# Routed experts of an AdaLN block on one core: one wait per gather and per adding scatter on GpSimd, the scatters' order kept by ScalarE, the expert register loaded one block ahead

## What is computed

```
scores = softmax(x @ gate_w.T)                      # 16 experts
topk_w, topk_ids = top_k(scores, 6); topk_w /= topk_w.sum()
for each expert e:  out += c_e[:, None] * (silu(x @ w1_e.T) * (x @ w3_e.T)) @ w2_e.T     # width 176
out += swiglu(x, shared weights)                     # width 352
result = x + gb * out
```

## Time and profile before

| | us |
|---|---|
| runs, median of 2 (lowest, highest) | 730.74 (729.31, 732.18) |
| profiled execution, its time | 729.74 |
| profiled execution, span from first to last instruction | 727.9 |
| busy in that span: TensorE / VectorE / ScalarE / GpSimd | 657.0 / 389.5 / 346.7 / 496.0 |
| mean granted TensorE clock | 0.95 |

### The profile page before, as it was taken

The page is one execution under the profiler, slowest core; times in us unless marked ns, Lnnn a source line. Parts: engine busy times, 40 slices in busy tenths (PEclk is TensorE's granted clock), DMA queues, the critical chain, the costliest instruction groups (busy, mean ns, idle before and its releaser), DMA issues.

```text
span 727.9 us, 13620 instructions
## 1 busy us (share of the span) xinstructions
PE 657.0 (90%) x4053; PEld 477.9 (66%) x4053; DVE 389.5 (54%) x1240; ACT 346.7 (48%) x886; POOL 496.0 (68%) x455
## 2 busy tenths in 40 slices
PE   8999997999989999965899999999999999999904
PEld 7889996999879988744565655555555555555503
DVE  6988779989777867897323222222222222222206
ACT  4788798989989654210244432332233233223300
POOL 4578878770876310598787888888788787878640
PEclk8999999999999999986899999999999999999965
DMA  8000001393001129100355555555555555554459
GB/s 308 2 1 1 2 1 45 103 322 88 2 1 37 38 77 288 37 13 0 92 91 82 86 87 86 84 86 90 82 85 89 86 82 88 90 82 84 67 82 314
DMA packets 55716, 61.55 MB, mean 85 GB/s; under 512 B 7800, under 2 KB 49024, under 8 KB 55520
## 3 DMA queue, kind: packets, MB, share of 16 engines
q0 software_dynamic: 21312, 30.02, 25.4%
q1 hardware_dynamic: 33920, 30.07, 13.4%
q10 hardware_dynamic: 416, 0.59, 0.2%
HBM read 37.18 MB, written 23.48 MB: 83 GB/s over the span
## 4 chain that ended last, share of the span: by engine, by line
PE 44%; POOL 24%; issue 15%; DMA 7%; DVE 4%; ACT 3%; SPq 1%; POOLq 0%; DVEq 0%; ACTq 0%
POOL xg L678 9%; PE ps L1453 7%; POOL routed L684 6%; POOL qoh L671 6%; DMA routed<-yb,idx 5%; PE ps L1097 4%; PE ps L1470 3%; PE ps L1303 3%; PE ps L1469 2%; PE ps L1444 2%; PE ps L1224 2%; PE ps L1248 2%; PE ps L1235 2%; PE ps L1249 2%; PE ps L1264 2%
## 5 line engine op out<-in xcount | busy, mean ns | idle before, releaser
L684 POOL DMA_INDIRECT routed<-yb,idx x111 | 176.0, 1586 | 39.3 <-issue 31.1
L1979 DVE SCALAR_TENSOR_TENSOR sw<-sil,cwt,ps 128x176 f32<-128x176 f32 x111 | 44.1, 398 | 250.9 <-ACT sil L986 250.9
L1453 PE MATMUL ps<-up_w,gT 128*128 x444 | 159.7, 483 | 8.2 <-ACT gT L980 4.1
L992 ACT ACTIVATE yb<-ps 128x256 f32<-128x256 f32 x111 | 42.7, 384 | 211.0 <-DMA routed<-yb,idx 188.4
L678 POOL DMA_INDIRECT xg<-token_rows,idx x111 | 110.6, 996 | 37.4 <-issue 30.2
L1453 PEld LDWEIGHTS ps<-up_w,gT 128*128 128x128 f32 x444 | 76.4, 192 | 49.8 <-issue 26.2
L1470 PE MATMUL ps<-dn,swT 48*128 x222 | 77.3, 428 | 0.0
L1469 PE MATMUL ps<-dn,swT 128*128 x222 | 66.4, 381 | 1.6 <-ACT yb L992 1.6
L671 POOL TENSOR_SCALAR qoh<-iota,blkf,tokn 128x112 f16<-128x112 f16 x48 | 40.8, 864 | 35.9 <-DVE blkf L1886 35.9
L986 ACT ACTIVATE sil<-ps,zero 128x176 f32<-128x176 f32 x111 | 45.6, 411 | 25.5 <-PE ps L1453 25.5
L1470 PEld LDWEIGHTS ps<-dn,swT 48*128 48x128 f32 x222 | 32.7, 184 | 36.8 <-issue 36.8
(11 more groups left out here) (275 smaller groups left out, 1418.6 us busy)
## 6 DMA issues: line engine op xcount, KB each, us to landing
up_w<-in_moew SPq DMA_DIRECT2D x4, 1408.0 KB, 12.7
routed<-zrow SPq DMA_DIRECT2D x2, 2176.0 KB, 16.2
accb<-routed SPq DMA_DIRECT2D x8, 512.0 KB, 8.1
wog<-combine SPq DMA_DIRECT2D x2, 1024.0 KB, 6.8
token_rows<-hxb SPq DMA_DIRECT2D x8, 256.0 KB, 2.2
out<-x1T SPq DMA_DIRECT2D x8, 256.0 KB, 2.3
xg<-token_rows,idx POOLq DMA_INDIRECT x111, 2.8
routed<-yb,idx POOLq DMA_INDIRECT x111
```

Source lines behind the costliest of these rows:

```text
L684: po.indirect_dma_start(acc_d[k % 2][:, :], bass.IndirectOffsetOnAxis(ap=idx[:, k:k + 1], axis=0), yb[:, k % Y_BUFS, :], None, compute_op= ...
L1453: last = mm(up_block(j), gT[:, j % 2, kc, :], up_w[:, kc, :, bass.ds(expert[j], 1), :], start=(kc == 0), stop=(kc == KC - 1))
L1979: ve.scalar_tensor_tensor(out=sw[:, j % 2, 0:I], in0=sil[:, j % 2, :], scalar=cwt[:, j % 4:j % 4 + 1], in1=up_block(j)[:, 1, :], op0=ALU.m ...
```

## The change

Four edits. `fetch(i)` has one wait in place of two: for `sw` of block i-6 (`s_a`), which comes after `x_t` and `c_ok` of that block. `add_rows(k)` has one wait in place of two: for `yb` k alone. ScalarE's yb(j) waits, from j = 2 on, for the landing of scatter j-2 in place of scatter j-4, and so keeps the order that `add_rows` kept before. TensorE loads the expert's register of block j+1 behind the up matmuls of block j, and not ahead of those of block j+1.

```
             def fetch(i):
                 if i >= XG_BUFS:
-                    po.wait_ge(*late("x_t", i + 1 - XG_BUFS))
-                    po.wait_ge(*late("c_ok", i + 1 - XG_BUFS))
+                    po.wait_ge(*late("s_a", i + 1 - XG_BUFS))
                 po.indirect_dma_start(xg[:, i % XG_BUFS, :], None, hx_d[:, :], ...)

             def add_rows(k):
                 po.wait_ge(*late("s_y", k + 1))
-                if k >= 2:
-                    po.wait_ge(S[f"sc{k % 2}"], 16 * (k // 2))
                 po.indirect_dma_start(acc_d[k % 2][:, :], ..., yb[:, k % Y_BUFS, :], None, compute_op=ALU.add)...

                     ac.wait_ge(*late("s_dn", j + 1))
-                    if j >= Y_BUFS:
-                        ac.wait_ge(S[f"sc{j % 2}"], 16 * ((j - Y_BUFS) // 2 + 1))
+                    if j >= 2:
+                        ac.wait_ge(S[f"sc{j % 2}"], 16 * (j // 2))
                     ac.activation(yb[:, j % Y_BUFS, :], bank(6 + j % 2)[:, 0:D], ACT.Copy).then_inc(S["s_y"], 1)

-            expert = {}
+            expert = {0: pe_.value_load(tab[0:1, 0:1], min_val=0, max_val=E - 1)}
...
                 if 0 <= j < NB:
-                    expert[j] = pe_.value_load(tab[j:j + 1, 0:1], min_val=0, max_val=E - 1)
                     pe_.wait_ge(*late("g_t", j + 1))
...
                     last.then_inc(S["s_up"], 1)
+                    if j + 1 < NB:
+                        expert[j + 1] = pe_.value_load(tab[j + 1:j + 2, 0:1], min_val=0, max_val=E - 1)
```

## The result

The changed kernel takes 768.23 us (median of two executions, 765.53 and 770.93) against 730.74: 1.052 times as long, 95% interval 1.0477 to 1.0564. Five further rounds gave 771.44 (769.99 to 774.76) against 729.45: 1.0575, 1.0545 to 1.0604. The direction and the mechanism were as forecast; the size was not. The range of 741 to 768 ends just under the first median and 3 us under the second, and the profiled execution (770.93) is 41.2 us over the one before (729.74) where the sum said 26.9.

The account below looks back on a forecast made before the run. GpSimd's own 3.19 us per block was taken as the bound. Start +3.7, loop +24.8 and end -1.6 summed to 26.9 us on the profiled 729.74, or 756.6; the forecast was 757 us, range 741 to 768.

Parts of the forecast that it names:

- What bounds the kernel before: Mid loop, GpSimd is its own bound: scatter 1.59, gather 1.00, two gaps of 0.30, 3.19 us per block; TensorE needs 2.79.
- Second waits for nothing: Taking second waits off GpSimd's 222 gathers and scatters gains 0 us each; the 0.30 us gap stays.
- The single wait at 0.29: On GpSimd, a gather with one wait starts 0.29 us after `sw` is done, priced from scatter 0.
- Rival C: The gather's single wait for `sw` costs 0.74 us, not 0.29: 780 us, chance 0.09.
- The register load at nothing: Moving 111 register loads on TensorE's queue one block ahead costs 0 us, within its 0.4 us slack per block.
- The ring: From yb(j) through gT, Silu, `sw`, gather, scatter, landing to yb(j+2): 6.88 us, 3.44 per block; chance 0.72.
- which wait gates: ScalarE's wait for the landing gates, with GpSimd idle 0.25 us per block ahead of the gather, for `sw`.
- The start: Up to scatter 2: gather 9 waits for `sw` 3, so scatter 2 starts at 368.76 instead of 365.06, +3.7 us.
- Scatter started to the yb that its landing releases, mean 3.90: Mid-loop time from scatter start to released yb: 3.81, 3.82, 4.08, mean 3.90 us; lower end 3.7, upper 4.08.
- the ordinary turn: One pass over two blocks, forecast at 6.88 us; 49 of them from scatter 2 to scatter 100 gave +24.8 us.
- The end: Scatter 100 to 110: 23.5 us instead of 25.1, -1.6, the last four pairs at 4.54 us each.
- Rival B: The landing seen is queueing behind gathers and falls to 2.8 us, no change: 728 to 731 us, chance 0.09.

## Why the prediction was right or wrong

*What bounds the kernel before* held. GpSimd's own 3.19 us is the pace in every kernel with an open ring.

*Second waits for nothing* held: the gap is 0.30 with one wait and with two.

*The single wait at 0.29* held: 0.27 measured. Rival C's 0.74 is right for a separate wait (0.75).

*The register load at nothing* held.

*The ring* held in all its links: it needs both new waits, it goes away with one block more, and its pace doubles with one block less (6.85). The statement on which wait gates held too: GpSimd waits for `sw` and ScalarE for the landing. The start was 0.2 us off.

*"Scatter started to the yb that its landing releases, mean 3.90"* is the step that failed. The typical pair is 3.89, but the mean over the loop is 4.04, for 12 of 97 are long. And since the excess of either chain of blocks holds up both, its 14.7 us count in full, 0.30 per turn, as if every pair took 4.19. Three pairs from one 10 us stretch could not show an event that comes every 25 us. I took their largest, 4.08, for an upper end, and that is too low for such a tail. More pairs of that trace would hardly have been enough: from scatter 2 to 98 it has two late landings (4.5 and 4.2 us). Other traces with an open ring have more, at no cost in time (the register load alone has six, up to 5.7). The question that was missing is what runs every few blocks beside the ring and at which moment of it. That is the loop's 12 of the 14.3 us; the ordinary turn, 6.85 for 6.88, took 1.5 back.

*The end* was 2.3 us off. The landing of scatter 99 is one of the late ones (5.2 us), which put scatter 101 at 4.58 behind scatter 100 and not at 3.44. Also GpSimd idled 1.67 us ahead of scatter 104 with nothing in the profile to say for what; the kernel before idled 2.59 us ahead of the same scatter, which the sum with its four equal pairs left out. What holds it there remains open.

*Rival B* asked whether the landing is queueing that goes when the queue is less loaded. It isn't: at half the DMA load, with the ring one block shorter, the median is the same 3.8 us. The estimate of 2.30 us worked out from the fit of the Trainium skill (DMA: Bandwidth & Descriptors, "Anatomy of one DMA — SWDGE (gpsimd) path") is therefore not the price of an adding scatter of 128 rows here; the shortest landing in the changed kernel is 3.6 us.

## What to carry to other kernels

When a wait is moved to another engine or put on a later event, walk the instructions queued behind it until you come back to it, and count the blocks that the walk spans: its length over that count is a pace of its own, and here one block more or less in the lag between gathers and scatters meant 730, 770 or 1103 us. A wait whose semaphore is "long fulfilled" in the trace before says nothing about the ring that it closes after. And once a DMA's landing is on the path, price it by its tail as well: long landings cost nothing in the kernels at 730 us and about their full excess here.

## What the hardware showed that was not expected

TensorE's instruction list comes in by DMA during the loop: packets of 16 KB, 14 over 98 blocks, 17 with twelve instructions more per block. The Trainium skill, Runtime: NRT & Kernel Launch, section "Instruction fetch mechanics", says that a sequencer refills in blocks of 16 KiB (256 instructions) through a DMA queue of its own and that crossing such a boundary is mostly hidden. The trace agrees with the size. In the kernel before they cost no time. In the changed one they are not hidden: 12 of the 14, which start 2.2 to 3.5 us behind an adding scatter, came with a landing 0.9 to 1.9 us over the median of 3.8, so the cost falls on another engine's DMA.

On GpSimd, a wait that goes with an indirect DMA let it start 0.27 us after the signal, and the same wait as an instruction of its own 0.75 us after. Where GpSimd had other work meanwhile, neither showed.
